# Decoder layer on one core: the blocks of probabilities transposed as two halves of 64 rows, into two banks

## The reference, cut to what matters

```python
x = _layernorm(x + _L0_attn_ref(x, w_q, w_k, w_v, w_o))
x = _layernorm(x + _L0_xattn_ref(x, ctx, ctx, mask, Wq, bq, Wk, bk, Wv, bv, Wo, bo))
x = _layernorm(x + _L0_ffn_ref(x, router_w0, wg0, wu0, wd0, router_w1, wg1, wu1, wd1))
```

## Time and profile before

| | |
|---|---|
| median of three executions | 4497.11 us (4495.11 to 4508.62) |
| the profiled execution | 4491.85 us, span of its records 4490.1 us |
| granted TensorE clock over the span | 0.99 of full speed |
| busy: TensorE, its weight loads | 4356.7 us (97%), 3811.3 us (85%) |
| busy: VectorE, ScalarE, GpSimd | 3698.2 (82%), 3259.8 (73%), 2742.9 us (61%) |
| 2048 self and 2048 cross transposes, TensorE | 265.1 and 288.1 us busy |

### The profile page before, as it was taken

How to read it: one execution, slowest core, us unless ns; L and a number is a source line. 1 busy time by engine, 2 the same in 40 slices (tenths; PEclk the granted TensorE clock), 3 DMA queues, 4 the chain that set the end, 5 groups by cost and what they waited for, 6 DMA issues and landing times. The chain is left out here.

```text
span 4490.1 us, 137989 instructions
## 1 busy us (share of the span) xinstructions
PE 4356.7 (97%) x42944; PEld 3811.3 (85%) x42944; DVE 3698.2 (82%) x18057; ACT 3259.8 (73%) x12741; POOL 2742.9 (61%) x3747
## 2 busy tenths in 40 slices
PE   7999999999999999999999999999995999999998
PEld 6988888888888888888888888888883778878886
DVE  4888888888888888888888888888886466658888
ACT  5888888888888888888888888888883444444444
POOL 3466666666666666666656666666566555557777
PEclk9999999999999999999999999999997999999999
DMA  5122121211221212112112111222215699988999
GB/s 170 48 71 67 67 69 65 66 65 63 73 67 65 69 65 66 65 64 73 66 66 68 65 66 65 66 71 67 68 60 162 203 342 342 318 279 284 310 307 290
DMA packets 477453, 552.60 MB, mean 123 GB/s; under 512 B 55632, under 2 KB 408144, under 8 KB 476240
## 3 DMA queue, kind: packets, MB, share of 16 engines
q1 hardware_dynamic: 350800, 296.21, 20.6%
q0 software_dynamic: 52224, 146.87, 8.7%
q10 hardware_dynamic: 73728, 100.70, 7.4%
HBM read 266.21 MB, written 277.35 MB: 121 GB/s over the span
## 5 line engine op out<-in xcount | busy, mean ns | idle before, releaser
L898 ACT ACTIVATE prob<-prob,negmax 128x128 f32<-128x128 f32 x2048 | 796.7, 391 | 299.4 <-DVE negmax L1032 299.4
L898 ACT ACTIVATE xprob<-xprob,xnegmax 128x128 f32<-128x128 f32 x2048 | 798.9, 400 | 3.8 <-DVE xnegmax L1032 3.8
L1364 POOL DMA_INDIRECT y_d<-y,to x576 | 563.6, 979 | 357.6 <-DVE y L1506 332.3
L1032 DVE CUSTOM_DVE_ANT_0 prob<-bank,causal 128x128 f32<-128x128 f32 x2048 | 452.8, 285 | 273.9 <-PE bank L787 248.8
L634 POOL DMA_INDIRECT xs_d<-xrow,place x512 | 554.9, 1084 | 133.4 <-issue 131.7
L1417 PE MATMUL bank<-moe,xgT 128*128 x2304 | 595.9, 382 | 2.6 <-issue 2.4
L597 POOL TENSOR_TENSOR rs<-spread_v,minus_half 128x1 f32<-128x1 f32 x256 | 146.7, 573 | 635.0 <-DVE spread_v L1106 634.8
L1080 DVE TENSOR_TENSOR xprob<-xprob,xinv 128x512 f32<-128x512 f32 x512 | 489.6, 956 | 17.5
L580 POOL CAST yTh<-yT 128x512 fp32r<-128x512 f32 x256 | 205.6, 803 | 431.9 <-ACT yT L934 431.9
L685 PE MATMUL bank<-xT0h,wqkv 128*128 128x256 f32 x2048 | 438.7, 298 | 19.4 <-DVE wqkv L434 11.3
L1032 DVE CUSTOM_DVE_ANT_0 xprob<-bank,xmask 128x128 f32<-128x128 f32 x2048 | 451.1, 284 | 0.3 <-PE bank L787 0.3
(11 more groups left out here) (174 smaller groups left out, 13330.7 us busy)
## 6 DMA issues: line engine op xcount, KB each, us to landing
xg<-xs_d SPq DMA_DIRECT2D x576, 129.0 KB
xs_d<-blank SPq DMA_DIRECT2D x248, 272.0 KB
rows<-y_d ACTq DMA_DIRECT2D x256, 256.0 KB
xT_s<-xT SPq DMA_DIRECT2D x128, 128.0 KB, 2.6
cT<-cT SPq DMA_DIRECT2D x128, 128.0 KB, 2.1
x_s<-x SPq DMA_DIRECT2D x128, 128.0 KB
x_d<-x SPq DMA_DIRECT2D x128, 128.0 KB, 1.9
sums<-x_d ACTq DMA_DIRECT2D x128, 128.0 KB
```

Source lines behind the costliest of these rows:

```text
L898: last = nc.scalar.activation(dst[:, h, :], dst[:, h, :], ACT.Exp, bias=src_bias[:, h:h + 1], scale=-1.0, accum_out=acc[:, h:h + 1])
L1032: last = nc.vector.tensor_tensor_reduce(dst[:, h, :], heads(h), bias[:, :], -1.0, float("inf"), ALU.add, ALU.min, least[:, h:h + 1])
L1364: nc.gpsimd.indirect_dma_start(y_d[:, :], bass.IndirectOffsetOnAxis(ap=to[:, m % NTO:m % NTO + 1].bitcast(U32), axis=0), y_s[q][:, :], Non ...
```

## The change

Each head is transposed in two halves of 64 rows (tokens that ask): rows 0 to 63 with the upper half of the identity go to the first bank of the pair, rows 64 to 127 to the second. A bank then holds 64 columns of each of eight heads, where it had 128 columns of four. The halves of a head follow each other, and the groups for self and cross attention stand next to each other in both kinds of double step. The waits are made once for eight heads. ScalarE copies a bank into one half of the columns of every head.

```diff
-            def four(a, side):
+            def half_of(a, side):
-                return a[:, side * PH:(side + 1) * PH, :].rearrange("p h q -> p (h q)")
+                return a[:, :, side * P // 2:(side + 1) * P // 2]
+
+            def eight(bank):
+
+                return bank[:, :].rearrange("p (h q) -> p h q", h=GH)
...
-                    def turn(n, side):
+                    def turn(n):
                         if not live(n - 1):
                             return
-                        pe.wait_ge(normed, 2 * (n - 1) + side + 1)
-                        if side == 0:
-                            masked_out(n, 0)
+                        pe.wait_ge(normed, 2 * n)
+                        masked_out(n, 0)
                         if not live(n):
-                            wait(pe, probT_in, 2 * (n - 2) + side + 1)
-                        for i in range(PH):
-                            last = nc.tensor.transpose(SCORES[side][:, i * P:(i + 1) * P], prob[:, (n - 1) % 2, side * PH + i, :], ident[:, :])
-                        last.then_inc(turned, 1)
+                            wait(pe, probT_in, 2 * (n - 1))
+                        for h in range(GH):
+                            for side in (0, 1):
+                                half = slice(side * P // 2, (side + 1) * P // 2)
+                                last = nc.tensor.transpose(SCORES[side][:, h * P // 2:(h + 1) * P // 2], prob[half, (n - 1) % 2, h, :], ident[half, half])
+                                if h == GH - 1:
+                                    last.then_inc(turned, 1)
...
                             job(n, "qk1")
-                            turn(n, 0)
-                            turn(n, 1)
-                            cross_turn(n, 0)
+                            turn(n)
+                            cross_turn(n)
                             job(n, "x1t")
-                            cross_turn(n, 1)
                             job(n, "v1")
...
                             job(n, "o1")
-                            turn(n, 0)
-                            turn(n, 1)
+                            turn(n)
+                            cross_turn(n)
                             job(n, "route")
                             job(n, "qk3")
-                            cross_turn(n, 0)
-                            cross_turn(n, 1)
                             job(n, "xk")
...
-                            nc.scalar.copy(four(probT, side), SCORES[side][:, :]).then_inc(probT_in, 1)
+                            nc.scalar.copy(half_of(probT, side), eight(SCORES[side])).then_inc(probT_in, 1)
```

More of the change, by code:

```diff
@@ L789, in cross_score, with cross_turn @@
                         last.then_inc(xscores, 1)
-                    def turn(n, side):
+                    def turn(n):
                         if not live(n - 1):
                             return
-                        pe.wait_ge(normed, 2 * (n - 1) + side + 1)
-                        if side == 0:
-                            masked_out(n, 0)
+                        pe.wait_ge(normed, 2 * n)
+                        masked_out(n, 0)
                         if not live(n):
-                            wait(pe, probT_in, 2 * (n - 2) + side + 1)
-                        for i in range(PH):
-                            last = nc.tensor.transpose(SCORES[side][:, i * P:(i + 1) * P], prob[:, (n - 1) % 2, side * PH + i, :], ident[:, :])
-                        last.then_inc(turned, 1)
-                    def cross_turn(n, side):
+                            wait(pe, probT_in, 2 * (n - 1))
[5 more added lines that the diff above has]
+                                    last.then_inc(turned, 1)
+                    def cross_turn(n):
                         x = n - CROSS
@@ L808, in cross_turn @@
                             return
-                        pe.wait_ge(xnormed, 2 * (x - 1) + side + 1)
-                        if side == 0:
-                            masked_out(n, 1)
+                        pe.wait_ge(xnormed, 2 * x)
+                        masked_out(n, 1)
                         if not live(x):
[L813 to L816, removed]
+                            wait(pe, xprobT_in, 2 * (x - 1))
+                        for h in range(GH):
+                            for side in (0, 1):
+                                half = slice(side * P // 2, (side + 1) * P // 2)
+                                last = nc.tensor.transpose(SCORES[2 + side][:, h * P // 2:(h + 1) * P // 2], xprob[half, (x - 1) % 2, h, :], ident[half, half])
+                                if h == GH - 1:
+                                    last.then_inc(xturned, 1)
                     def mix(n):
@@ L925, in move_cross_turned @@
                             act.wait_ge(xturned, 2 * x + side + 1)
-                            nc.scalar.copy(four(xprobT, side), SCORES[2 + side][:, :]).then_inc(xprobT_in, 1)
+                            nc.scalar.copy(half_of(xprobT, side), eight(SCORES[2 + side])).then_inc(xprobT_in, 1)
                     def move_y(n):
```

## The result

The changed kernel takes 4474.39 us (median of 6 runs, 4470.44 to 4478.96) against 4496.11 of the kernel before on the same chip (4493.23 to 4508.62): a ratio of 0.9947, 95% interval 0.9934 to 0.9961. It is faster, by 22 us where 69 were forecast. The profiled execution took 4474.03, its span is 4472.3.

The account below looks back on a forecast made before the run. TensorE, busy 996 of 1000 us, was taken as the bound until another engine is late. Gains of 0.48 + 0.13 + 0.36 + 0.13 = 1.10 us, over 63 pairs of batches, make 69 us: 4428, range 4370 to 4482.

Parts of the forecast that it names:

- The transposes: Self and cross blocks on TensorE: 16 rounds of 0.057 us plus 0.35 for tile changes, 1.26 for 1.74.
- step D: Odd double step in which x is split, 13.93 us before: all of the 0.48 us gained.
- Rival 1: Transposes on TensorE: a half costs what a whole does, so slower, 4587 us; chance 0.11.
- Even steps: Even double steps, 12.19 us: VectorE's row up to the copy of x1T bounds them, so only 0.13 gained each.
- step A: Even double step behind the split of x: forecast to gain 0.13 us, bound by x1T.
- C: The other even double step, behind the late odd one: forecast to gain 0.13 us, bound by x1T.
- the floor: Even steps: xq can't start sooner than some 0.14 us behind the end of x1T's copy.
- The wait of the cross turn: Even steps: new waits of the cross transposes for the cross normalisation (xprob), 0.1 to 0.2 us each.
- The late odd step B: Odd double step held by GpSimd's chain from x's low half to root: 0.36 us gained, bounds 0.1 and 0.6.
- rival 3: VectorE and GpSimd take most back; even steps and the late odd one gain nothing: 30 us, 4467; chance 0.16.

Follow-up runs that it names:

- act_first: Kernel after, with ScalarE emptying qk1's bank ahead of the copies of the self blocks in even steps; step A 12.44 us for 12.90, B 14.25 for 13.52.
- scatter_late: Kernel after, with GpSimd's two indirect scatters of even steps moved behind open_blocks, root and x1b: 4396.78 us, ratio 0.9786.
- order_only: Changed kernel with whole blocks of 128 rows again, keeping its order and waits: ratio 1.0002 to the kernel before; with the scatters late too, 0.9960.
- scatter_early: Kernel after, with the scatters right behind the split of y, ahead of spread_keys, on GpSimd: 4490 us.
- one_inc: Kernel after, with only a group's last transpose signalling, one count in place of two: neither the lateness nor the time changed.
- x1t_between: Kernel after, with x1's transposes between self and cross groups in even steps: interval overlaps the kernel after's; with the scatters late too, 0.9806.

## Why the prediction was right and wrong

**The transposes: right.** Within a group the rounds come 0.062 us apart, for 0.057. Both loads of a pair go on beside the streams, at 138 ns (self) and 140 ns (cross), for 141. Route starts 1.14 us behind the first transpose; the first itself starts 0.09 later behind o1 than before (0.21 for 0.12), and what follows route starts 0.10 later behind it (0.47 for 0.37). That makes 1.33 for 1.26, and 0.41 less than 1.74, which is what step D gained. Of the 1.33, 16 rounds are 0.99, so entering and leaving the tiles cost 0.34, where I had 0.35: the rounds are what I had too short. (The 0.22 to 0.29 above is less because a group's slow first round, 0.05 more than the others, is counted to the group there.) Rival 1 (a half costs a whole) is out: it needed rounds of 0.087.

```profile
L806 PEld LDWEIGHTS bank<-ident,prob 64*128 64x128 f32 x4096 | 147.5, 138 | 39.7 <-issue 5.6
```

Pairs of loads start every 0.062 us though the profile shows each at 138 ns, so one pair keeps the next out for no more than 0.062. The Trainium skill's rule in "TensorE: Matmul & The Clock Gate" (LDWEIGHTS) has P/1.2 ns for a load, 0.107 us for one of 128 columns. An estimate by that rule: a round would last 0.107 at least, and the block be longer than before. The measurement decides against it here.

**Odd step D: right.** 13.93 to 13.51, 0.42 for 0.48.

**Even steps: the step that failed.** I had them gain 0.13 each, "whatever the transposes save", with x1T as their one bound, and I had put ScalarE's copies at nothing since the engine is idle 0.95 and 0.87 us. In step A the copies came 1.2 us late, more than that cover, and pulled qk1's move and xq with them (xq at +9.32 for +8.89), and the cross mix behind it: a loss of 0.71. In C x1T was the bound, as I had it: xq started 0.12 sooner (+8.80 for +8.92). But its matmuls, which now follow a wait, took 0.97 to the next group for 0.89, which I had not counted, and the step gained 0.04. The order of the queue (self copies, then the bank that xq needs) was in the code, but no row of before had the word to ScalarE late, and I did not ask what TensorE's new spacing would fall beside on GpSimd. With the scatters out of the way the mechanism holds: 12.19 to 11.98, 0.20 for 0.13, and xq starts 0.15 behind the end of x1T's copy (below; xq at 1050.68 in the lines above), the floor that I had taken. The wait of the cross turn for the normalisation that I had forecast for even steps came as well: its group starts 0.67 (A) and 0.79 (C) behind the self group, in odd steps 0.55.

```profile
1050.12 0.41 DVE L1092 COPY x1T<-bank 128x256 f32<-128x256 f32 x1
```

**The late odd step B: right chain, wrong amount (the second step that failed).** It gained 0.84 for 0.36, but only because A in front of it ran 0.71 longer and GpSimd's chain had that much more time; act_first took 0.46 of A's loss away and B gave 0.73 back. The pair A and B is what that chain holds: 0.13 gained of a forecast 0.49. This is rival 3 in its amount, in one half of the steps: VectorE and GpSimd take it back. Rival 3's price (30 us, 4467) is also the nearest to the result, 7 us from it. Its condition, that B and the even steps gain nothing, holds roughly for their sum (0.17 of 0.62) but for neither A nor B alone, and the late word, which the runs show for A, isn't in its reason. The result lies inside the range that I gave, 4370 to 4482, but 46 us from my 4428.

**The sum.** 0.42 (D) + 0.04 (C) + 0.13 (A and B) = 0.59 (0.58 before rounding) for 1.10 us a pair of batches. Over the attention, from the first self scores to the last, the profiled executions differ by 25.8 us: some 36 from the steady steps, less 1.6 in one of the first (11.58 for 10.03) and 4.6 in the last three, which is told below; some 4 are in the short first steps and in stray ones. The expert stage is 7 us longer in this one profiled execution (1123.1 for 1115.9 behind the last scores), 2.6 in that of scatter_late. It doesn't go with the halves: it took 1123.6 in order_only, with whole blocks, and 1115.0 in scatter_early, with halves. Why it differs is not known, and no experiment was made for it.

**What stays open.** Why an indirect scatter holds the word that TensorE's transposes are done. In every kernel tried, late words lie beside or just behind the second scatter, and moving it later or earlier makes them punctual. But a scatter beside them isn't enough: in the kernel before, too, it runs while the words fall due (1022.14 for 1.25 us), and the copies still begin at 1022.81, 0.97 behind their group. Two rivals are out: two increments in place of one (one_inc), and that TensorE goes straight on to the cross group (x1t_between has other work there, and the word is as late; the kernel before goes straight on to four cross blocks, and it is punctual). In order_only, whole blocks in the new order, it is late in most even steps and on time in a few. What decides wasn't found.

## What to carry to other kernels

Price a faster piece of TensorE's program together with what it will then stand beside: here GpSimd's queue held back some 43 of the 64 us that the halves can bring, and moving two scatters behind the one result that VectorE waits for gave three times the gain of the change itself (0.0161 of the time for 0.0053; on the kernel before, where no word was late, the move gave 0.0064). Run the change again once the next engine is out of the way, on both kernels, before judging it: 22 us became 64. And put the work of one tile shape side by side; here a lone group in 64-row tiles gave most of its gain back at the two switches.

## What was not expected of the hardware

**A late word beside a scatter.** In even steps the copy that waits for TensorE's group starts 0.87 us behind the group's first transpose with the scatters moved away, and 2.05 in the median (2.37 at most) beside the second scatter in step A of the kernel after, while the group behind it on TensorE starts as in scatter_late (0.67 behind the first, L822 at 1016.42 in the lines above).

**The clock in the last steps.** At the end of the attention the last three double steps of the kernel after take 14.70, 13.45 and 14.30 us; before they take 12.17, 13.46 and 12.17. In windows over the last three steps (before, then after) the granted clock, third number from the end, is 1.00 throughout before and 0.77, 1.00 and 0.76 after:

```profile
3336.40:3348.60 12.20, 10.01 (x118) 7.74 (x112) 9.51 (x56) 9.44 (x40) 9.02 (x16) 1.00 0.09 30
3348.60:3362.10 13.50, 11.95 (x141) 9.90 (x137) 11.95 (x65) 10.55 (x44) 6.20 (x7) 1.00 0.28 93
3362.10:3374.20 12.10, 9.92 (x116) 7.72 (x112) 9.66 (x57) 9.34 (x40) 9.02 (x16) 1.00 0.09 28
```
```profile
3306.90:3321.60 14.70, 11.86 (x130) 9.57 (x131) 9.70 (x57) 9.63 (x41) 9.03 (x16) 0.77 0.08 27
3321.60:3335.00 13.40, 11.24 (x153) 9.24 (x154) 11.86 (x63) 10.45 (x44) 6.17 (x7) 1.00 0.28 91
3335.00:3349.20 14.20, 11.76 (x130) 9.41 (x130) 9.62 (x57) 9.53 (x40) 9.02 (x16) 0.76 0.08 26
```

These steps have less work, and in two of them TensorE idles ahead of the self transposes in both kernels alike (3.7 us in all for VectorE's masking, 1.9 at the longest). The kernel after idles a further 0.97 and 0.56 us ahead of the cross transposes of these two, where the kernel before goes straight on. It was at the lower of the clock's two levels (1.2 GHz) for a part of both, and the three steps took 4.6 us longer. scatter_late, granted 0.87 to 0.89 in its last three steps, pays 4.4 us against the kernel before with the scatters late, and order_only with the scatters late, at 1.00, pays nothing (12.13, 13.44, 12.15). But the halves are not needed for it: order_only, with whole blocks and the scatters where they were, was granted 0.88 in its last step, which took 13.77 us for 12.17. The kernels with halves all have such a step. What brings the clock down there and not elsewhere was not tried.
